# Masking half of a cross-attention's scores with matmuls before the exponential, in place of a minimum after it

## The reference, cut to what matters

```python
x = x + _L2_xattn_ref(_layernorm(x, axis=-1), ctx_1024, ctx_1024, mask_1x1xSxS2_bk1, ...)

def _L2_xattn_ref(query, key, value, mask, W_q, W_k, W_v, W_o):
    Q = _split(query @ W_q.T)          # 32 x 16 heads x 64 queries x 8
    K = _split(key @ W_k.T)            # 32 x 16 heads x 1601 keys x 8
    V = _split(value @ W_v.T)
    scores = jnp.einsum('bhqd,bhkd->bhqk', Q, K) / jnp.sqrt(jnp.float32(D_K))
    scores = jnp.where(mask, -jnp.inf, scores)     # mask: 1 x 1 x 64 x 1601, the same for all samples and heads
    attn_w = jax.nn.softmax(scores, axis=-1)
    attn_w = jnp.nan_to_num(attn_w, nan=0.0)
    out = jnp.einsum('bhqk,bhkd->bhqd', attn_w, V)
    ...
    return merged @ W_o.T
```

## Time and profile before

| what | value |
|---|---|
| three runs | 3685.76, 3703.05, 3704.51 us; median 3703.05 |
| the profiled execution | 3703.05 us |
| its span, first to last instruction | 3701.1 us |
| granted TensorE clock, mean of the span | 0.847 |
| PE, DVE, ACT, POOL busy, share of the span | 75%, 64%, 38%, 12% |
| the layer `L2_xattn` in the span | about 1173 to 2492 us |

### The profile page before, as it was taken

The page is one execution under the profiler, slowest core; times in us unless marked ns, Lnnn a source line. Parts: engine busy times, 40 slices in busy tenths (PEclk is TensorE's granted clock), DMA queues, the critical chain, the costliest instruction groups (busy, mean ns, idle before and its releaser), DMA issues. The chain is left out here.

```text
span 3701.1 us, 64502 instructions
## 1 busy us (share of the span) xinstructions
PE 2761.4 (75%) x26142; PEld 1728.9 (47%) x26142; DVE 2379.7 (64%) x6735; ACT 1406.6 (38%) x2463; POOL 425.7 (12%) x275
## 2 busy tenths in 40 slices
PE   7866643696897999999999999984554557887723
PEld 4655532454664455555555555551111224565412
DVE  4433312475112399999999999956999853444776
ACT  3431211363333255555555555523111122443521
POOL 2310011240000000000000000000445400001300
PEclk9995766797998599999999999956777767899966
DMA  7740032000000001010101010001122100552000
GB/s 167 175 109 0 14 88 59 7 3 14 18 17 25 27 20 28 20 29 20 28 20 29 20 27 21 2 7 49 72 109 91 46 12 6 138 135 52 9 0 12
DMA packets 206584, 159.45 MB, mean 43 GB/s; under 512 B 11778, under 2 KB 195045, under 8 KB 202160
## 3 DMA queue, kind: packets, MB, share of 16 engines
q1 hardware_dynamic: 205264, 153.48, 15.0%
q0 software_dynamic: 1024, 1.85, 0.2%
HBM read 151.09 MB, written 4.46 MB: 42 GB/s over the span
## 5 line engine op out<-in xcount | busy, mean ns | idle before, releaser
L2745 DVE CUSTOM_DVE_ANT_0 L_xattn_junk<-L_xattn_ps_mx,L_xattn_shift 128x512 f32<-128x512 f32 (+1 forms) x1024 | 544.6, 569 | 114.7 <-issue 111.7
L2791 DVE TENSOR_TENSOR L_xattn_pT<-L_xattn_pT,L_xattn_capT 128x512 f32<-128x512 f32 (+1 forms) x896 | 542.3, 646 | 31.6 <-ACT L_xattn_pT L2826 26.7
L2826 ACT ACTIVATE L_xattn_pT<-L_xattn_ps_st 128x512 f32<-128x512 f32 x768 | 416.9, 594 | 348.4 <-PE L_xattn_ps_st L2610 348.4
L2623 PE MATMUL L_xattn_ps_mx<-L_xattn_kT,L_xattn_qb 32*128 32x512 f32 (+1 forms) x2048 | 513.3, 571 | 1.1 <-DVE L_xattn_tops L2745 0.7
L2610 PE MATMUL L_xattn_ps_st<-L_xattn_qb,L_xattn_kT 32*128 32x256 f32 (+1 forms) x3328 | 457.0, 389 | 0.0
L2610 PEld LDWEIGHTS L_xattn_ps_st<-L_xattn_qb,L_xattn_kT 32*128 32x128 f32 (+1 forms) x3328 | 310.4, 186 | 22.8
L2656 PE MATMUL L_xattn_ps_pv<-L_xattn_pT,L_xattn_v 128*17 128x128 f32 x6656 | 271.5, 283 | 0.0
L2656 PEld LDWEIGHTS L_xattn_ps_pv<-L_xattn_pT,L_xattn_v 128*17 128x17 f32 x6656 | 149.7, 98 | 170.5 <-DVE L_xattn_pT L2791 126.6
L1785 DVE SCALAR_TENSOR_TENSOR x<-L_ffn_ps_o,L_ffn_weights,x 128x128 f32<-128x128 f32 x128 | 36.0, 344 | 224.3 <-PE L_ffn_ps_o L1698 224.3
L2623 PEld LDWEIGHTS L_xattn_ps_mx<-L_xattn_kT,L_xattn_qb 32*128 32x128 f32 x2048 | 168.5, 189 | 12.5 <-DVE L_xattn_tops L2745 9.8
L2636 PE MATMUL L_xattn_ps_st<-L_xattn_less,L_xattn_ones_b 3*128 3x512 bf16 x768 | 167.2, 394 | 1.7 <-ACT L_xattn_pT L2826 1.4
(11 more groups left out here) (548 smaller groups left out, 5298.0 us busy)
## 6 DMA issues: line engine op xcount, KB each, us to landing
L_xattn_ctx<-in_ctx SPq DMA_DIRECT2D x96, 768.0 KB
L_attn_bb<-scratch_rows SPq DMA_DIRECT2D x16, 1024.0 KB, 4.7
L_attn_cc<-scratch_rows SPq DMA_DIRECT2D x16, 1024.0 KB, 6.7
L_xattn_mask<-in_mask_keys SPq DMA_DIRECT2D x32, 400.2 KB, 6.9
L_ffn_w<-in_L_ffn_w SPq DMA_DIRECT2D x32, 256.0 KB, 3.1
L_ffn_w<-in_L_ffn_W SPq DMA_DIRECT2D x16, 256.0 KB, 3.2
L_xattn_mask<-in_mask_pairs SPq DMA_DIRECT2D x32, 100.1 KB, 4.5
L_xattn_ctx<-in_ctx SPq DMA_DIRECT2D x96, 32.5 KB
```

What stands on the lines that cost most here:

```text
L2623: last = nc.tensor.matmul(mx[:, w % 3, to:to + width], qb[n % 3][32 * g:32 * g + 32, 2 * (p % 2):2 * (p % 2) + 2, :].rearrange("p h q -> p ...
L2745: last = nc.vector.tensor_tensor_reduce(out=junk[:, w % 3, to:to + width], in0=mx[:, w % 3, to:to + width], in1=shift[:, k0:k0 + width], s ...
L2791: nc.vector.tensor_tensor(x, x, capT[0:k, j[0]:j[1], :].unsqueeze(2).broadcast_to([k, j[1] - j[0], 4, S]), ALU.min)\
L2826: nc.scalar.activation(pT[b % HELD][:, :, gi, :], st[:, w % 3, :].rearrange("p (c k) -> p c k", c=2), ACT.Exp)\
```

## The change

In even bundles (half 0) masked scores are no longer set to zero by a minimum after the exp. PE adds twice -2^100 to them before the exp, with bf16 matmuls: the stationary operand is a block of the mask's rows (`bounds`, 32 queries x 128 keys), the moving one has a one where a column belongs to that query (`places_b`, 32 x 256). Since 64 queries don't fit into 32 rows, it takes two (i = 0, 1) for each block and group. Odd bundles keep the minimum. The values of a bundle are multiplied one bundle earlier, and `pT` has 5 buffers in place of 7. The start loads and converts the operands of the new matmuls: ten more DMAs, and four more operations on DVE ahead of the layer norm. In GpSimd's part the loop is only written otherwise.

```diff
+        masks = [s.sb(f"mask{i}", [P, KEYS], U8) for i in (0, 1)]
+        bounds = [s.sb(f"bounds{i}", [P, KEYS], BF16) for i in (0, 1)]
+        places, places_b = [s.sb(f"place{i}", [P, S]) for i in (0, 1)], [s.sb(f"place_b{i}", [P, 4, S], BF16) for i in (0, 1)]
-        pT = [s.sb(f"pT{u}", [P, 2, 2, 256]) for u in range(HELD)]
+        pT = [s.sb(f"pT{u}", [P, 2, 2, 256]) for u in range(5)]
...
-            return [x for x in (b - 4,) if x % ROUND == 0 and 0 <= x < BUNDLES] + \
-                [x for x in (b - 3,) if x % ROUND and 0 <= x < BUNDLES]
+            return [x for x in (b - 3,) if x % ROUND == 0 and 0 <= x < BUNDLES] + \
+                [x for x in (b - 2,) if x % ROUND and 0 <= x < BUNDLES]
...
+            for i in (0, 1):
+                sp.dma_start(places[i][:, :], a["c_thirty_two"][i]).then_inc(loaded, 16)
+                for g in range(GROUPS):
+                    sp.dma_start(masks[i][32 * g:32 * g + 32, :], a["mask_all"][32 * i:32 * i + 32, :]).then_inc(loaded, 16)
...
-            pe.wait_ge(loaded, 144)
+            pe.wait_ge(loaded, 304)
...
+            def no_bounds(b, n, step, half, i, c2):
+
+                j = 2 * step + c2
+                if j >= KC:
+                    return
+                for gi in (0, 1):
+                    w, r = 2 * b + gi, 32 * (2 * half + gi)
+                    nc.tensor.matmul(st[0:chunk[j], w % 3, 256 * c2:256 * c2 + 256], bounds[i][r:r + 32, P * j:P * j + chunk[j]],
+                                     places_b[i][r:r + 32, :, :].rearrange("p h q -> p (h q)"), start=False, stop=False,
+                                     tile_position=(r, 0))
...
-                pe.wait_ge(capped, 2 * b + 2)
+                if half:
+                    pe.wait_ge(capped, b + 1)
+                else:
+                    pe.wait_ge(exped, 2 * b + 2)
...
                 if now:
+                    for i in (0, 1) if now[2] == 0 else ():
+                        no_bounds(b, *now, i, 0)
+                        no_bounds(b, *now, i, 1)
                     keys_by_query(b, *now, 0)
                     keys_by_query(b, *now, 1)
...
             nc.vector.tensor_scalar(cap[:, :], mask[:, :], -2.0, 2.0, ALU.mult, ALU.add)
+            for i in (0, 1):
+                nc.vector.tensor_scalar(bounds[i][:, :], masks[i][:, :], 2 * OUT, None, ALU.mult)
+                nc.vector.tensor_copy(places_b[i][:, :, :], places[i][:, :].unsqueeze(1).broadcast_to([P, 4, S]))
...
-                if now:
+                if now and now[2]:
                     step = now[1]
                     for gi in (0, 1):
...
-                n, off = divmod(b - ROUND - 2, ROUND)
+                n, off = divmod(b - ROUND - 1, ROUND)
...
-                    if b >= HELD and gi == 0:
-                        act.wait_ge(pv_done, b - HELD + 1)
+                    if b >= 5 and gi == 0:
+                        act.wait_ge(pv_done, b - 4)
```

More of the change, by code:

```diff
@@ L2463, in many_head_cross_attention @@
     LEAD = 18
-    HELD = 7
     FIRST, LAST = -LEAD - ROUND, ROUND * (B - 1) + ROUND + 10
@@ L2570, in _ @@
             nc.gpsimd.memset(parts[:, :, :, :], 0.0).then_inc(filled, 1)
-            pool.wait_ge(loaded, 144)
-            def own_queries(n):
+            pool.wait_ge(loaded, 304)
+            for n in range(B):
+                if n == 0:
+                    pool.wait_ge(*V.at("q3"))
                 if n >= 3:
@@ L2578, in own_queries @@
                                         four[:, :].unsqueeze(2).broadcast_to([P, 4, S]), ALU.mult).then_inc(qb_made, 1)
-            pool.wait_ge(*V.at("q3"))
-            for n in range(3):
-                own_queries(n)
-            for n in range(3, B):
-                own_queries(n)
         @block.tensor
@@ L2656, in values @@
                         last = nc.tensor.matmul(pv[32 * q:32 * q + 17, P * half:P * half + P], v[n % 3][0:chunk[j], j, 4 * half + q, :],
-                                                pT[b % HELD][0:chunk[j], c2, q // 2, P * (q % 2):P * (q % 2) + P],
+                                                pT[b % 5][0:chunk[j], c2, q // 2, P * (q % 2):P * (q % 2) + P],
                                                 start=False, stop=(j == KC - 1 and half == 1), tile_position=(0, 32 * q))
@@ L2719, in _ @@
         def _(dve):
-            dve.wait_ge(loaded, 144)
+            dve.wait_ge(loaded, 304)
             nc.vector.tensor_scalar(shift[:, :], mask[:, :], OUT, None, ALU.mult)
             nc.vector.tensor_scalar(cap[:, :], mask[:, :], -2.0, 2.0, ALU.mult, ALU.add)
+            for i in (0, 1):
+                nc.vector.tensor_scalar(bounds[i][:, :], masks[i][:, :], 2 * OUT, None, ALU.mult)
+                nc.vector.tensor_copy(places_b[i][:, :, :], places[i][:, :].unsqueeze(1).broadcast_to([P, 4, S]))
             nc.vector.memset(zero_b[:, :], 0.0).then_inc(V.did("set"), 1)
@@ L2788, in _ @@
                         k, j = (P, (2 * step, 2 * step + 2)) if step < 6 else (KREST, (KC - 1, KC))
-                        x = pT[b % HELD][0:k, 0:j[1] - j[0], gi, :].rearrange("p c (h q) -> p c h q", q=S)
+                        x = pT[b % 5][0:k, 0:j[1] - j[0], gi, :].rearrange("p c (h q) -> p c h q", q=S)
                         dve.wait_ge(exped, 2 * b + gi + 1)
@@ L2822, in exps @@
                     act.wait_ge(scored, w + 1)
-                    if b >= HELD and gi == 0:
-                        act.wait_ge(pv_done, b - HELD + 1)
+                    if b >= 5 and gi == 0:
+                        act.wait_ge(pv_done, b - 4)
                     if step < 6:
-                        nc.scalar.activation(pT[b % HELD][:, :, gi, :], st[:, w % 3, :].rearrange("p (c k) -> p c k", c=2), ACT.Exp)\
+                        nc.scalar.activation(pT[b % 5][:, :, gi, :], st[:, w % 3, :].rearrange("p (c k) -> p c k", c=2), ACT.Exp)\
                             .then_inc(exped, 1)
                     else:
-                        nc.scalar.activation(pT[b % HELD][0:KREST, 0, gi, :], st[0:KREST, w % 3, 0:256], ACT.Exp).then_inc(exped, 1)
+                        nc.scalar.activation(pT[b % 5][0:KREST, 0, gi, :], st[0:KREST, w % 3, 0:256], ACT.Exp).then_inc(exped, 1)
             def taken(unit):
```

## The result

The changed kernel takes 3732.46 us, median of 5 runs (3729.46 to 3734.45), against 3703.05 us (3685.76 to 3705.09) before: a ratio of 1.0089, 95% interval 1.0065 to 1.0112. It is slower, by 29 us between the medians (33 us by the ratio), and inside the predicted range of 3725 to 3795, near its lower end. The times of the kernel before fall into two groups, in its later runs 24 of 64 at 3679 to 3687 us with a mean granted clock of 0.851 to 0.855 and 40 at 3693 to 3705 with 0.846 to 0.850, and its profile, at 3703, is one of the upper group. The profiled execution of the changed kernel has a span of 3732.0 us, 30.9 more than before.

What follows compares the result with a forecast made beforehand. PE was taken as the bound, through its chain of scores. Masks +82.6, clock at 0.50 +4.3, waits -43.5 and start +8.5 gave +51.9 us on 3703.05: 3755 us, range 3725 to 3795.

Steps and rivals of the forecast that it cites:

- What bounds the kernel: Middle of the layer: PE is the bound, its chain of scores alone setting 1.18 us of each bundle.
- The added masks, +82.6 us at 0.43 per bundle: Six even bundles in each of 32 rounds: four 256-column matmuls per row group lengthen PE's chain by 0.43 us.
- The wait at position 10: Bundle 10 of a 14-bundle round: PE's 1.20 us idle before the T transposes goes entirely, 28 times, -33.6 us.
- Position 4: Bundle 4 of a round: PE's 0.33 us wait for ACT's exps goes as values move earlier, 30 times, -9.9 us.
- The earlier values give PE no time back: Values one bundle earlier, 5 pT buffers: no new waits, about 1 us of room, nothing gained on PE.
- The start, +8.5 us: Layer start: ten more DMAs on SP's queue, 5.7 us, and four DVE operations before the layer norm, 2.8 us.
- The tail, +9.5 us: First bundle and tail run at a clock of 0.50: some ten even bundles' masks cost +4.3 us more.
- a small one: Last 60 us: more work on PE may keep the clock at 1.00 longer, worth 10 us at most.
- Rival 1: Added mask matmuls: their weight loads show, twice 0.43 us per bundle, +87 us, 3842 us; chance 0.08.
- Rival 2: Position 10: the wait stays since DVE's chain to x hardly moves, +33.6 us, 3789 us; chance 0.10.
- Rival 3: Even bundles: masks are hidden beside the maxima and the waits still go, -35 us, 3668 us; chance 0.08.
- rival 4: Even bundles: an addition of about 0.18 to 0.25 us, halfway, so no change, 3703 to 3715 us; chance 0.07.

Runs made afterwards that it cites:

- experiment 1: Two kernels from the changed one: without the added mask matmuls, 3645.76 us; with every mask matmul issued twice, 3815.31 us.

## Why the prediction was right, point by point

**What bounds the kernel.** Right. PE's first part is set by the chain of scores, and what is put in front of it shows there in full (experiment 1).

**The added masks, +82.6 us at 0.43 per bundle.** Right: 0.439. For rounds 0 to 29 that is 79 us where 77 were forecast. The row that decided it was the scores' spacing in the earlier trace rows, whose 0.43 us are 256 columns in two passes, 0.215 each. The Trainium skill, TensorE: Matmul & The Clock Gate, Part 3 (The mechanism), has a weight load overlap only matmuls of another row group; by that the even bundle's first part would have been 1.18 + 2 x 0.43 = 2.04 us with one set. It was 1.622, so this pattern of matmuls doesn't pay for its loads; PEld has a span of 0.09 us for each of them.

**The wait at position 10, -33.6 us.** Right: 1.165 us a round where 1.20 were forecast. The forecast of 0.1 us to spare was a little generous, since 0.04 us of waiting are left in the mean (0.598 against 0.562 for values without a wait); with so little room it is partly luck that nearly all went. Only 0.75 us of it go with the minima (1.763 to 1.009 without masks), the other 0.41 are filled by the masks. The forecast's working has that as well: with nothing added, x would be done at 1686.15 - 0.43 = 1685.72 and PE there at 1685.42, 0.30 us of waiting, and 0.45 was measured.

**Position 4, -9.9 us.** Right: 0.323 us, and the kernel with the values moved alone has all of it.

**Not in the forecast.** Moving the values also gave 0.20 us at position 3, where the zeroing matmul overlaps the scores, and the masks filled 0.06 us of a wait at position 8, which the values alone leave as it was (0.626 us from values to prepare in both kernels, 0.561 with masks). 0.26 x 30 = 8 us, about what the forecast of the rounds (+33.9) has over the measurement (+25.9). "The earlier values give PE no time back" is the step that failed here: it followed the waits, and not which instruction comes next behind the scores.

**The start, +8.5 us.** The mechanism was right, the terms were too large. The mask DMAs of 32 rows took 0.46 us each and not 0.59, the copies to bf16 cost 0.2 to 0.25 and not 0.42; the layer norm begins 6.2 us later, not 8.5. Of these only 4.0 reach the first less_max, since the clock stood at 1.00 for 6.8 us (1202.4 to 1209.3) where before it did for 3.4 (1198.9 to 1202.3): the last projections of the queries and the first two groups of transposes of ctx ran in it, and the delay falls to 4.9 us in front of these transposes and to 4.0 behind them.

**The tail, +9.5 us and "a small one".** Here the forecast had the sign wrong. The two last rounds hold the masks' 5.2 us, but the clock stayed at 1.00 to 2465 where before it was at 0.50 from 2411 to 2417 and from 2428 on. The whole came to -6.8: 16 us less than the sum, not 10 at most. It isn't a property of the change that can be relied on. From the start of round 30 to the last addition to x the kernel with the values earlier took 78.8 us, and the same kernel with the addition to x first, which does the same work, 88.2; the clock first fell 35 us into that stretch in the one and 22 in the other. The kernel before by itself has times 14 us apart at mean clocks of 0.852 and 0.847. What makes the clock fall earlier or later I didn't find.

**Behind the layer, +7.8 us.** The code there is the same. The mean granted clock of this part is 0.767 before and 0.758 after; why it differs is open. Over the whole span it is 0.847 and 0.848.

**The rivals.** Rival 1 (weight loads) falls with 1.622 and 2.059. Rival 2 (the wait stays) falls with the earlier trace rows's 31.7 us gone to 0.1, though by a hair. Rival 3 (masks hidden) holds for position 12 alone, and rival 4 (half of the cost) falls with 1.622 too.

**The sum.** Measured less forecast: -8.0 in the rounds, -4.5 at the start, -16.3 in the tail, +7.8 behind the layer. They left 31 of the 52 us forecast for the profiled execution (29 by the medians). So the direction and the cost of the masks were forecast for the right reason, and the sum was two thirds too high. The last two parts, -8.5 us together, move with the clock and were luck, good or bad; without them the time would be some 3741 us, in the range as well.

## What to carry to other kernels

Two engines at 94% in the same stretch aren't both the bound: compare like parts of the slower one's timeline at different operand sizes, and see which chain sets each. Work taken from the other engine is worth only the waits that end on it, here 27 us for 271, so take away the one operation that such a wait stands behind, and look up in the trace whose it is before building; here one bundle's masks or four minima put later in the queue shortened the round by 0.79 and 0.50 us, where the whole change lengthened it by 0.89. An operation put ahead of another moves the wait to what the other releases, so the order has to be judged to the end of the round.

## What the runs showed of the hardware that was unexpected

- bf16 matmuls of 32 rows by 256 columns follow each other in one row group at 0.110 us at a clock of 1.00, and two groups do so side by side (sixteen in 0.87 us); their weight loads (128 columns each, 0.09 us on PEld) don't show.
- A matmul whose row groups are free starts while earlier ones run in others: the zeroing matmul of pv at 1679.92, and the last scores, begun at 1679.62, take until 1680.21 by their entry.
- GpSimd's product of 128 x 512 fp32 took 1.27 us by its span where it was shortest (spans on GpSimd are rough), 1.8 times DVE's minimum of the same shape (0.69). The mean is 1.63, since beside DVE's minima one of the two waits: GpSimd's product took 2.00 us, or DVE's minimum 1.76.
- In that kernel PE was idle for 1.3 to 1.4 us fifteen times in the middle of the layer, and thirteen times the granted clock fell from 1.00 to 0.50 within 2 us behind it, for 3.4 or 6.8 us.
- The granted clock at the layer's end fell for good at 2428 us in one kernel and at 2465 in the other, and the end of the layer differs by 9.4 us between two kernels that do the same work there.
